# A Mamba-attention-MoE block on one core: the scan's engine programs in another order, and two small power passes a chunk made one

## The reference, cut to what matters

```
xn = (x - mean) * rsqrt(var + 1e-5) * ln_w + ln_b          # over channels
z, xBC, dt = split(xn @ in_proj)                            # 256, 320, 8
xBC = silu(conv3x3(xBC) + conv_b)                           # depthwise
y   = ssd(xs * dt, dt * A, B, C, chunk=128) + D * xs        # 8 chunks an image
y   = y * silu(z)
y   = y * rsqrt(mean(y*y) + 1e-5) * rms_w                   # "norm factor", one a token
t   = x + y @ out_proj
# then the attention takes (t - mean(t)) / sqrt(var(t) + 1e-5)   # "reciprocal deviation", one a token
```

## Time and profile before

| | us |
|---|---|
| median of 3 runs | 2355.66 |
| the three runs | 2348.87, 2355.66, 2388.62 |
| the profiled execution | 2352.81 |
| its span (first to last instruction) | 2351.1 |
| PE busy in the span | 2128.0 (91%) |
| DVE busy | 1647.6 (70%) |
| POOL busy | 1572.3 (67%) |
| ACT busy | 1274.3 (54%) |
| mean granted TensorE clock | 0.944 |

### The profile page before, as it was taken

One profiled execution on the slowest core, in us unless ns is written; L12 is line 12 of the kernel. 1 busy time (PEld: TensorE's weight loads), 2 busy tenths in 40 slices (PEclk: granted clock), 3 DMA queues, 4 the chain that ended last, 5 costly groups with the idle time before them and its releaser, 6 DMA issues. The chain is left out here.

```text
span 2351.1 us, 40009 instructions
## 1 busy us (share of the span) xinstructions
PE 2128.0 (91%) x11907; PEld 1738.3 (74%) x11907; DVE 1647.6 (70%) x4242; ACT 1274.3 (54%) x2623; POOL 1572.3 (67%) x1599
## 2 busy tenths in 40 slices
PE   4698999898996999999999999999999993799994
PEld 2466666666765888888888888888888882688883
DVE  4768887887756677777877778778777773344444
ACT  3646655665532666666666666666666661233331
POOL 2679888988852666687686776867858675355551
PEclk9989999899987999999999999999999996899996
DMA  1950000000001001010010010100101001455555
GB/s 59 387 193 10 10 10 1 10 1 1 19 1 28 1 1 26 2 39 6 6 39 2 21 24 3 43 1 10 36 1 42 4 7 42 172 193 191 196 174 215
DMA packets 135402, 130.94 MB, mean 56 GB/s; under 512 B 82885, under 2 KB 101359, under 8 KB 135190
## 3 DMA queue, kind: packets, MB, share of 16 engines
q1 hardware_dynamic: 124950, 107.12, 14.9%
q0 software_dynamic: 9088, 17.07, 2.1%
q10 hardware_dynamic: 1152, 4.19, 0.4%
HBM read 64.78 MB, written 65.10 MB: 55 GB/s over the span
## 5 line engine op out<-in xcount | busy, mean ns | idle before, releaser
L1224 POOL TENSOR_TENSOR plo<-pf,phi 128x512 fp32r<-128x512 f32 (+1 forms) x640 | 752.0, 1186 | 339.4 <-ACT phi L1452 306.8
L1450 ACT ACTIVATE pf<-psum 128x512 f32<-128x512 f32 (+1 forms) x640 | 357.1, 558 | 412.9 <-PE psum L1285 308.0
L1452 ACT ACTIVATE phi<-psum 128x512 fp32r<-128x512 f32 (+1 forms) x640 | 355.1, 555 | 0.0
L1596 DVE CUSTOM_DVE_ANT_0 psum<-psum,ahead_wide 128x128 f32<-128x128 f32 (+3 forms) x512 | 246.7, 502 | 69.2 <-PE psum L1338 67.3
L1283 PE MATMUL psum<-phi,x_tok 128*128 128x512 f32 (+1 forms) x640 | 265.8, 415 | 5.8 <-POOL plo L1224 5.8
L1877 POOL DMA_INDIRECT chosen<-yg,xg x156 | 152.8, 979 | 153.2 <-DVE yg L1989 115.1
L1338 PE MATMUL psum<-xT,qT 128*128 128x512 f32 (+3 forms) x768 | 244.5, 346 | 4.8 <-DVE peak L1596 3.3
L1283 PE MATMUL psum<-qT,xT 128*128 128x512 f32 (+1 forms) x640 | 237.9, 372 | 1.9 <-ACT phi L1452 1.3
L1284 PE MATMUL psum<-plo,x_tok 128*128 128x512 f32 (+1 forms) x640 | 237.7, 371 | 0.0
L1285 PE MATMUL psum<-phi,x_tok 128*128 128x512 f32 (+1 forms) x640 | 237.6, 371 | 0.0
L1284 PE MATMUL psum<-qT,xT 128*128 128x512 f32 (+1 forms) x640 | 236.6, 370 | 0.0
(11 more groups left out here) (293 smaller groups left out, 5285.4 us busy)
## 6 DMA issues: line engine op xcount, KB each, us to landing
wg<-turned_w SPq DMA_DIRECT2D x39, 874.0 KB, 4.6
routed<-empty SPq DMA_DIRECT2D x1, 34056.0 KB, 95.9
xg<-routed SPq DMA_DIRECT2D x39, 264.0 KB, 4.2
qT<-nmax SPq DMA_DIRECT2D x512, 0.5 KB, 2.0
y<-chosen SPq DMA_DIRECT2D x8, 1024.0 KB, 10.2
turned_w<-wT SPq DMA_DIRECT2D x8, 874.0 KB, 4.4
x_in_sb<-in_x SPq DMA_DIRECT2D x8, 512.0 KB, 3.4
out<-o_st ACTq DMA_DIRECT2D x8, 512.0 KB, 5.7
```

The costliest lines, as they stand in the source:

```text
L1224: g_.tensor_tensor(plo[:, T % RP, 0:n], pf[:, T % RF, 0:n], phi[:, T % RP, 0:n].bitcast(F32), ALU.subtract).then_inc(a["low_ready"], 1)
L1450: s_.activation(pf[:, T % RF, 0:n], bank[T % RS][:, 0:n], ACT.Exp)
L1452: s_.activation(phi[:, T % RP, 0:n], bank[T % RS][:, 0:n], ACT.Exp).then_inc(a["high_ready"], 1)
L1596: last = v.tensor_tensor_reduce(out=source[:, col:col + n], in0=source[:, col:col + n], in1=ahead_wide[:, HALF - n:HALF], scale=1.0, scala ...
```

## The change

The arithmetic stays. Two things are different.

First, `chunk_rs` and `chunk_rs2` become one call. ACT now writes the mean square of chunk g+1 beside the variance of chunk g, in a third column of `mv`, and POOL makes both factors with one addition and one power over two columns. The call stands where `chunk_rs2` stood, after the fade. So a chunk's norm factor is made at the end of POOL's step s, not at its start, and DVE's `chunk_t` wants it at the start of step s+1 as before.

Second, all orders are redrawn. PE: `chunk_seg` and the z projection come before `chunk_turn`; `chunk_y` comes before `turn_back`, `project(nn, 0)` and `chunk_out`. The z quarters are at j = 3, 4, 5, 7 (before: two at 3, one at 4, one at 5). ACT follows: decay before `chunk_out`, `tanh_bc` at 6 (before 5), `tanh_x(n, 1)` last in step 6, and in step 7 `pad_copy(nn, 0)` before `spread_bc`. DVE: taps 3, 3, 3, 1, 2, 3, 3 at j = 0 to 6 (before 4, 4, 4, 2, 2, 2 at j = 0 to 5), both statistics at 3, before the tap. POOL: additions 2, 2, 2, 2 at j = 2 to 5 (before 2, 3, 3 at 2 to 4), `deviation` at 4 (before 5).

```diff
@@ POOL
+                    def chunk_rs(g):
+                        c0, c1 = (1 if g < 0 else 0), (2 if g + 1 < G else 1)
+                        need(pool, "mv_ready", g + 1)
+                        if g + 1 < G:
+                            pool.wait_ge(s["ssq_ready"], g + 2)
                         need(pool, "lnx_ready", g - 3)
+                        need(pool, "t_drained", g - 2)
+                        two = rs2[:, g % 4, c0:c1]
+                        g_.tensor_tensor(two, mv[:, g % 4, 1 + c0:1 + c1], epst[:, 0:1].to_broadcast([P, c1 - c0]), ALU.add).then_inc(s["ve_ready"], 1)
+                        pool.wait_ge(s["ve_ready"], g + 2)
+                        g_.tensor_tensor(two, two, mhalf[:, 0:1].to_broadcast([P, c1 - c0]), ALU.pow).then_inc(s["rs2_ready"], 1)
-                    ADDS = {2: range(0, 3), 3: range(3, 6), 4: range(6, 9)}
+                    ADDS = {2: range(0, 3), 3: range(3, 5), 4: range(5, 7), 5: range(7, 9)}
-                        if 0 <= step - 3 < G:
-                            chunk_rs(step - 3)
-                        if 0 <= step - 4 < G:
-                            chunk_rs2(step - 4)
+                        if -1 <= step - 4 < G:
+                            chunk_rs(step - 4)
-                        if has(nn) and j == 5:
+                        if has(nn) and j == 4:
                             deviation(nn)
@@ PE
                             chunk_in(step)
-                        if 3 <= step < G + 6:
-                            chunk_turn(step)
-                        if 0 <= step < G:
                             chunk_seg(step)
...
+                            if j == 5:
+                                project_z(n, 0)
+                            if j == 7:
+                                project_z(n, 1)
...
+                        if 3 <= step < G + 6:
+                            chunk_turn(step)
...
                             chunk_y(step - 1)
...
+                            if j == 6:
+                                turn_back(nn, 0)
+                            if j == 7:
+                                project(nn, 0)
+                        if 0 <= step - 3 < G:
+                            chunk_out(step - 3)
@@ ACT
-                        a_.activation(ysq[:, :], y1[:, g % 4, :], ACT.Square, scale=DI ** -0.5, accum_out=ssq[:, g % 4:g % 4 + 1]
+                        a_.activation(ysq[:, :], y1[:, g % 4, :], ACT.Square, scale=DI ** -0.5, accum_out=mv[:, (g - 1) % 4, 2:3]
...
-                            if j == 5:
+                            if j == 6:
                                 tanh_bc(n)
...
                         if has(nn) and j == 7:
                             pad_copy(nn, 0)
+                        if has(n) and j == 7:
+                            spread_bc(n)
...
+                        if has(n) and j == 6:
+                            tanh_x(n, 1)
@@ DVE
-                        dve.wait_ge(s["rs_ready"], g + 1)
+                        dve.wait_ge(s["rs2_ready"], g + 1)
...
-                    TAPS_AT = {0: ((0, range(0, 4)),), 1: ((0, range(4, 8)),), 2: ((0, range(8, 9)), (1, range(0, 3))),
-                               3: ((1, range(3, 5)),), 4: ((1, range(5, 7)),), 5: ((1, range(7, 9)),)}
+                    TAPS_AT = {0: ((0, range(0, 3)),), 1: ((0, range(3, 6)),), 2: ((0, range(6, 9)),), 3: ((1, range(0, 1)),),
+                               4: ((1, range(1, 3)),), 5: ((1, range(3, 6)),), 6: ((1, range(6, 9)),)}
```

More of the change, by code:

```diff
@@ L546, in _ @@
                                 project(n, 4)
-                            if j == 4:
-                                project_z(n, 0)
-                            if j == 5:
[L550 to L561, removed]
+                            if j == 5:
+                                project_z(n, 0)
+                            if j == 7:
+                                project_z(n, 1)
+                        if has(n - 1):
+                            if j == 3:
+                                project_z(n - 1, 2)
+                            if j == 4:
+                                project_z(n - 1, 3)
+                        if has(nn) and j == 2:
+                            residual(nn, 0)
+                        if 3 <= step < G + 6:
+                            chunk_turn(step)
                         small = None
@@ L742, in _ @@
                                 pad_copy(n, 4)
-                            if j == 4:
[L744 to L752, removed]
-                                normalise(nn, 0)
-                                normalise(nn, 1)
-                                turned_back(nn, 0)
+                            if j == 5:
+                                tanh_z(n, 0)
+                            if j == 7:
+                                tanh_z(n, 1)
+                        if has(n - 1):
+                            if j == 3:
+                                tanh_z(n - 1, 2)
+                            if j == 4:
+                                tanh_z(n - 1, 3)
+                        if has(nn) and j == 2:
+                            residual(nn, 0)
+                        if 3 <= step < G + 6:
+                            chunk_out(step)
+                        if has(nn) and j == 6:
+                            normalise(nn, 0)
+                            normalise(nn, 1)
+                            turned_back(nn, 0)
                         if has(n):
@@ L779, in _ @@
                                 pad_copy(n, 5)
-                        if has(n - 1) and j == 3:
-                            tanh_z(n - 1, 3)
                         if has(nn):
@@ L957, in _ @@
                             chunk_y(step - 2)
-                        if has(n - 1) and j == 4:
-                            gate_z(n - 1, 3)
                         if has(n):
@@ L964, in _ @@
                                 cumulated(n)
+                        if has(nn) and j == 3:
+                            statistics(nn, 0)
+                            statistics(nn, 1)
                         if has(n):
@@ L976, in _ @@
                             sums_apart(n)
[L977 to L978 removed]
+                        if has(n - 1):
+                            if j == 3:
+                                gate_z(n - 1, 2)
+                            if j == 4:
+                                gate_z(n - 1, 3)
                         if has(n):
[L980 removed]
+                            if j == 5:
                                 gate_z(n, 0)
[L982 removed]
+                            if j == 7:
                                 gate_z(n, 1)
[L984 to L988 removed]
         with ExitStack() as attn:
```

52 lines of the change are left out of this document (11 added, 41 removed).

## The result

The changed kernel takes 2368.6 us in the median of 20 runs, the kernel before 2352.7. The ratio, taken over undisturbed runs, is 1.0053 with a 95% interval of 1.003 to 1.0075: slower, by less than 2%. The forecast was 2351 us, a hair faster, so the time lies in the range and the sign is wrong. The profiled execution of the changed kernel took 2373.73 us (span 2372.0), so the two traces differ by 20.9 us, somewhat more than the medians (15.9).

A forecast was written before the change was run, and what follows sets the result against it. No engine fills the scan; PE is nearest: 66.0 us of work an image, 6.5 low clock, 6.05 idle. 2352.81 + 3.6 (six images) - 2.5 (opening) - 3 (last two images) = 2350.9, likeliest 2351 us; range 2318 to 2378.

The forecast's parts named there:

- The sum for an image: One scan image: 41.0, 18.1 and 18.2 us, together 77.3 at full clock, plus 1.7 for low clock: 79.0 instead of 78.4.
- the term for the low clock: PE in a scan image: 3.4 us at half level, charged as 1.7 us.
- the two large waits: PE in a scan image: half-clock stretches behind these stay in some form, one of them under POOL's lateness.
- the three parts of the forecast sum: PE's step 2 to the end of Xd in step 6, 41.0 us; chain to the next image, 18.1; steps 0 and 1, 18.2.
- The parts outside the pattern: Outside the repeating images: the opening at -2.5 us (between -6 and +2) and the last two images at -3.
- POOL's middle: POOL's steps 4 and 5 come to some 22 us; PE waits for Xd about 3 us in step 5 and 3 in step 6.
- one of the forecast's own signs of being wrong: The forecast is wrong if POOL has idle time in steps 4 and 5.
- The port: DVE taps meeting long POOL products: each product holds DVE up by at most 1.0 us, not by its whole length.
- The turn behind the exponents: PE's 3.3 us wait for DVE's L935 goes, and with it most of the low clock of step 3.
- The power made once: POOL's norm factors: two-column power 0.71 us, a chunk 1.0 instead of 1.6; worth something only where others wait for POOL.
- ACT in steps 6 and 7: Chain from the end of Xd in step 6 to PE's next image: 18.1 us, where it was 16.1.
- the slower one: Rival: low clock of 6.8 us behind each new PE wait for Xd; an image 82.4 us, total 2373 us; chance 0.16.

The follow-up runs named there:

- silu_late: The changed kernel with POOL's silu_x(n, 0) moved from the end of step 5 to the end of step 6, ahead of silu_bc: 2350.9 us.
- fill: The changed kernel with useless PE matmuls ahead of the wait for Xd, 4 in step 5 and 9 in step 6: 2357.7 us.
- turn_only: The kernel before with only chunk_turn moved behind the exponents and z, and ACT's chunk_out behind its exponential: 2469.5 us, ratio 1.0486.
- spread_first: The changed kernel with ACT's spread_bc ahead of pad_copy(nn, 0) in step 7, as in the kernel before: 2366.2 us.
- z_in_6: The changed kernel with the second z quarter (project_z, tanh_z, gate_z) in step 6 and not in step 7: 2368.1 us.
- mended_bare: The changed kernel with silu_x(n, 0) late, spread_bc first and the second z quarter in step 6, without filler matmuls: 2343.5 us.
- fill_tb: The kernel before with 8 useless PE matmuls ahead of turn_back in step 6: 2356.1 us, ratio 1.0014.
- all_mended: mended_bare plus 2, 4 and 6 useless PE matmuls ahead of the waits for Xd in steps 4, 5 and 6: 2336.1 us.

## Why the prediction was wrong

*The sum for an image, the term for the low clock.* This is the step that failed. The prediction charged 1.7 us. Measured in the image at 236.2 us it is 10.1, half of the 20.13 us in which PE worked at the half clock; before it was 6.5. Over the five images it is 9.9 on average (379.73 us of PE's busy time less five times 66.0). The idle time was over-charged in turn: 77.3 at full clock less 66.0 of work is 11.3 us, and PE was idle for 6.7. With 66.0 + 6.7 + 1.7 an image would take 74.4; it takes 82.8. I argued that the stretches "behind the two large waits stay in some form" and that one lies under POOL's lateness. They grew from 13.6 to 20.5 us, over steps 5, 6 and 7. One does lie under POOL's lateness: PE comes out of it at 293.4 and then waits for `Xd` until 297.15. Nothing hid the other 13.4 us, which cost 6.7. By the three parts of the forecast sum, the stretch up to the end of `Xd` in step 6 took 42.7 us against 41.0, the rest of steps 6 and 7 21.9 against 18.1, and steps 0 and 1 18.2 as forecast. One sign in the first part is wrong as well: the 0.4 us for one more tap's blocking was subtracted, where blocking adds; with it turned the part is 41.8.

*The parts outside the pattern.* The forecast counted six images at +0.6, the opening at -2.5 and the last two images at -3. In the traces the five images gave +21.3, the first image -6.8, the opening -1.5 and the last two +4.1. That the time still lies in the range is owed in part to the first image, whose gain no term stands for.

*POOL's middle.* Right in place and mechanism: PE waits for `Xd` in steps 5 and 6, 1.6 and 3.05 us, against about 3 and 3. silu_late and fill show that the loss hangs on it. Its size was too high: POOL is busy for 17.3 us of steps 4 and 5, which take 19.0, where 22 were forecast, and it is idle for 1.3 us of step 4, one of the forecast's own signs of being wrong.

*The port.* A tap costs DVE more when it meets a long POOL product than the 1.0 us that I took from the earlier trace rows: the longest tap is now 3.18 us, where 2.31 was the longest. It is the second tap of step 6, which began at 293.4, within `silu_x`.

```profile
L889 DVE SCALAR_TENSOR_TENSOR acc<-pad,cw,acc x128: 1329/1584/3182, 36.5 to 629.9; 128x1088 f32<-128x1088 f32 x128
```

That is 1.85 us over the minimum, near the 2.2 us of an undisturbed `silu_x`, so the Trainium skill's rule (SBUF — State Buffer, "Who interferes with whom") is nearer to the trace here than my reading of the rows was.

*The turn behind the exponents.* Its wait went and step 3 came down by 3.7 us, as forecast. turn_only shows what was not in the working: without `chunk_y` behind it the turn brings another wait in.

*The power made once.* 0.70 us for two columns while DVE is idle, against 0.71 forecast, and 0.78 in the median. It is worth 0 in the old orders and about 9 us in the new: it counts where POOL is waited for.

*ACT in steps 6 and 7.* From the end of `Xd` at 297.10 to PE's next image at 319.0 it was 21.9 us against 18.1.

```profile
297.10:319.00 21.90, 20.84 (x86) 14.94 (x87) 10.17 (x21) 11.55 (x24) 11.46 (x15) 0.69 0.00 1
```

PE is busy for 20.84 of the 21.9 us, at a granted clock of 0.69, and idle only for the wait of 1.0 us at the end, so for nearly all of it PE at the half clock set the pace and not the chain through ACT that the forecast added up. Shortening ACT's part was worth nothing while the waits for `Xd` stood (spread_first, z_in_6).

*The rivals.* The one that happened is the slower one, with a chance of 0.16: low clock behind PE's waits for `Xd`. It gave 82.4 us an image and 2373 us; the images are 78.0 to 86.5, 82.7 on average, and the time 2368.6. Its mechanism is what fill and mended_bare bear out. That its number fits so well is partly luck: it has 5.1 us of low clock an image where 10.1 were measured, on top of the same 77.3 that charges too much idle time, and its condition, over 2 us of wait in both steps, held in one of the two (1.6 and 3.05). What the chances had wrong is that the low clock was taken as a small correction to each case, when the profile of before already showed it to be as large as all idle time together, 6.5 us against 6.05.

What stays open: what sets off the half clock, in the old orders above all. In the new ones most of it goes when idle PE ahead of `chunk_y` is filled, which still doesn't say what in the mix of work and waits decides. fill_tb has it behind 23 us without a pause. By the Trainium skill (TensorE: Matmul & The Clock Gate, "HAM oscillation") it is PE's idle gaps that bring the clock down and unbroken work that holds it up; fill, all_mended and mended_bare agree with that, fill_tb does not.

## What to carry to other kernels

Where one engine is near its bound and its clock depends on what it does, count low-clock time as a term of its own, as large as the idle time, and ask of each new wait where it falls. Before moving a call, ask which wait it was covering: here the turn moved without `chunk_y` cost 4.9%, and `chunk_y` moved alone 1.2%. A cheap trial is worth more than a longer sum: three calls moved by a step or a place, and a dozen filler matmuls an image, made 1.4% between kernels that look alike (2368.6 and 2336.1 us).

## What the runs showed of the hardware that was not expected

The half clock came to a PE that was busy for 23.2 us on end (fill_tb, 225.0 to 248.2 us), so full occupation by the profile's count did not protect it; that stretch holds many narrow matmuls of 8 and 32 columns, but whether they matter was not tested. Filler of 128x32 by 128x256 did hold the clock up elsewhere: 0.95 with, 0.90 without, in the same orders. A convolution tap on DVE and a long product on POOL hold each other up by far more than the medians say: the tap that began within `silu_x` took 3.18 us, where one alone takes 1.33, and `silu_x` 3.66, where it takes 2.2 by itself.
